# A four-layer tower on one core: the state-space sub-block takes B, C and delta straight from its normed rows, through weights multiplied together on the chip

## The chip, the cores and the metric

One core of a Trainium2 chip runs the whole program in one launch. It has TensorE (PE in the profile, with PEld its weight loads), VectorE (DVE), ScalarE (ACT), GpSimd (POOL) and SyncE (SP), which issues the direct DMAs. The metric is the device time of one execution in microseconds; lower is better. Every engine runs its instructions in order, and orders itself against the others by semaphores.

## The reference, cut to what matters

The tower turns 16 images into 16 x 36 = 576 tokens of width 256 and adds eight sub-blocks to a residual stream, each on the layer-normed stream. The third one, `L1_attn`, is the one changed. Per token row `x_in` (256 wide):

```
xz = x_in @ W_in                  # W_in 256 x 512
x, z = (xz[..., :D], xz[..., D:])
proj = x @ W_x                    # W_x 256 x (256 + 2*16)
delta_raw = proj[..., :D]; B_ssm = proj[..., D:D + N]; C_ssm = proj[..., D + N:]
delta = jax.nn.softplus(delta_raw @ W_dt + b_dt)
A = -jnp.exp(A_log)
dA = exp(delta * A); dBx = delta * x * B_ssm
h = dA_t * h + dBx_t              # along the 36 tokens of an image, 16 states per channel
y = sum over states (h * C) + x * D_param
y = y * jax.nn.silu(z) @ W_out    # then a layer norm of y + x_in, scaled and shifted
```

The sub-blocks ahead of it are a tanh recurrence (`attn0`) and a mixture of eight experts, one chosen per token (`ffn0`); behind it stand another mixture (`ffn1`) and two more layers.

## The kernel before, in words

All sub-blocks are written out one behind the other, once in each engine's program. The residual stream H and its normed copy XH lie tokens-by-partition in five tiles (four of 128 tokens, one of 64). `transpose_x(name)` on PE and `xt_copy(name)` on ACT turn XH into XT, channels by partition (2 blocks of 128 x 576 tokens). The PSUM tensor PS has 8 banks of 512 columns. A product 576 tokens wide is made in two halves of 288, each of two accumulating matmuls (k = 0, 1); the trace shows two records for one f32 matmul.

*The end of attn0 and the start of ffn0.* PE makes `token_products("attn0")`. Then `normed_residual` on DVE takes statistics of y + x, a reciprocal square root (`rsqrt`: DVE adds epsilon and signals `var_ready`, ACT takes `Sqrt` in `square_root`, line 859, DVE finishes), scales and adds, takes statistics again, and two more such roots follow. ACT's queue has only these three roots here, behind two sines. Beside that PE runs `keep_warm(11, root=4)`: 11 turns of 4 products on a zero tile, whose result nobody reads, then it waits for the fourth root and runs 5 more. After it come `transpose_x("ffn0")`, the gate's logits, the ranks, and the routed experts.

*The state-space stage* (`attn1`). PE, DVE, ACT in the order of the program:

- PE: four products of XT with `win_s` (m = 0, 1 give x, m = 2, 3 give z), banks 4 to 7, signalled by `xz_psum`; ACT copies x to `xs` and takes SiLU of z into `zs` (line 992), signalling `xz_read`.
- PE: B and C from `xs` and the last 32 columns of `wx_s`; ACT copies them to `bc_s` (line 996). SP stores them in DRAM and loads each of the 32 rows back, spread over 128 partitions (`bcB`, `bcC`, four buffers each, lines 383 to 395).
- PE: `dr`, the product of `xs` with the first 256 columns of `wx_s`; ACT copies it (line 1000); PE: its product with `wdt_s`.
- Softplus as max(v, 0) + log(1 + e^-|v|), with a correction for the rounding of 1 + e: ACT Abs with the bias (line 1005), Exp (line 1008), Ln (line 1010); DVE from line 1524 on, at full width (1152 columns for both blocks of channels), ends in `dl` (delta) and `dx` (delta times x). ACT takes exp(A_log) at line 1012.
- The loop over 16 states: DVE `input_of` (line 1549, dx times B row) and two scans (line 1557, one for each block of channels), ACT the decays for a block (line 1022, into PSUM `dA`, banks 3 to 6), POOL the product of the states with the C row (line 1170), PE the sum over states in banks 0 to 2, by products with the identity; ahead of it PE puts x times D there (`diagD`).
- DVE multiplies by `zs` (line 1571), PE makes the token products with `wout_s`.

ACT evaluates its functions from tables; the trace has a separate ACT_TABLE_LOAD wherever the next function is in another set. Its line is that of the function that it stands ahead of.

## Time and profile before

| | us |
|---|---|
| median of 3 runs | 929.83 (927.01 to 931.51) |
| profiled execution | 929.02 |
| its span | 927.2 |
| PE busy | 800.0 |
| DVE busy | 351.2 |
| ACT busy | 253.5 |
| POOL busy | 134.7 |
| mean granted clock of PE | 0.922 of full speed |

The profile is one execution, taken by the hardware profiler; times in it count from the span's start. The end of the first sub-block lies at 83 to 108, the state-space stage at 241 to 348. Busy time is the sum of an engine's instructions; a busy PE includes the idle products. The chain of waits goes back from the last instruction to what released it; a piece of it is time in which nothing else could have made the program shorter.

### The profile page before, as it was taken

The numbers are of one execution on the slowest core, as the hardware profiler recorded it, in microseconds if no ns is written. First come the engines' busy times: TensorE is split into PE (matmuls) and PEld (weight loads), VectorE is DVE, ScalarE is ACT, GpSimd is POOL, SyncE is SP. The second block draws the span as 40 slices with busy tenths as digits, with TensorE's granted clock in tenths as the row PEclk, the third lists the DMA queues.
The fourth block names the chain that finished last, engine by engine and source line by source line (L and its number), as shares of the span: only waits on it lengthen the run. The fifth ranks groups of instructions, "written<-read, shape, count | busy, mean of one in ns | idle before, by whom it ended". The sixth has DMA issues, their size and how long they took to land.

```text
span 927.2 us, 13868 instructions
## 1 busy us (share of the span) xinstructions
PE 800.0 (86%) x4994; PEld 599.6 (65%) x4994; DVE 351.2 (38%) x994; ACT 253.5 (27%) x588; POOL 134.7 (15%) x100
## 2 busy tenths in 40 slices
PE   8878779999936669998869799999998988999995
PEld 5466449897523345564544468899874556999984
DVE  1335640000359967465627641111115641111113
ACT  1222114443243321453357121222220021222210
POOL 1000020001008960023003240000013030000004
PEclk9856889999977999798999989999999978999998
DMA  9500057994034510000200064899952042899952
GB/s 336 210 2 2 1 219 262 309 318 153 20 115 117 150 28 0 1 1 0 103 0 0 1 244 138 303 322 316 309 204 84 0 163 93 276 318 317 320 179 77
DMA packets 39590, 139.27 MB, mean 150 GB/s; under 512 B 5744, under 2 KB 20288, under 8 KB 27904
## 3 DMA queue, kind: packets, MB, share of 16 engines
q1 hardware_dynamic: 37312, 132.88, 42.7%
q0 software_dynamic: 2240, 5.90, 1.9%
q8 instruction: 22, 0.36, 0.2%
q14 instruction: 16, 0.13, 0.0%
HBM read 127.40 MB, written 11.35 MB: 150 GB/s over the span
## 4 chain that ended last, share of the span: by engine, by line
PE 60%; DVE 17%; DMA 8%; issue 6%; ACT 5%; POOL 1%; another core or an unknown queue 1%; SPq 0%; DVEq 0%; POOLq 0%; ACTq 0%
PE PS L418 58%; DVE arena L1557 4%; DMA arena<-w_moe 2%; DMA arena<-x_slots 2%; DVE stats L1238 1%; DMA arena<-y_slots,posu 1%; PE PS L475 1%; PE PS L441 1%; DMA arena<-w_down 1%; ACT arena L970 1%; DVE H L1394 1%; DMA x_slots<-XH,posu 1%; DVE stats L1231 1%; DVE arena L1661 1%
## 5 line engine op out<-in xcount | busy, mean ns | idle before, releaser
L418 PE MATMUL PS<-arena 128*128 128x128 f32 (+4 forms) x3308 | 412.7, 278 | 33.5 <-ACT arena L970 9.8
L418 PEld LDWEIGHTS PS<-arena 128*128 128x128 f32 (+2 forms) x3308 | 361.7, 172 | 73.5 <-issue 19.0
L418 PE MATMUL PS<-warm 128*128 128x512 bf16 (+1 forms) x556 | 130.9, 383 | 9.7 <-DVE rs L1222 9.0
L1382 DVE TENSOR_TENSOR arena<-arena,PS 128x384 f32<-128x384 f32 (+1 forms) x62 | 30.2, 488 | 207.7 <-ACT arena L907 207.7
L418 PEld LDWEIGHTS PS<-warm 128*128 128x128 bf16 x556 | 54.6, 101 | 76.3 <-DVE rs L1222 12.8
L1157 POOL DMA_INDIRECT arena<-y_slots,posu x25 | 23.8, 951 | 389.3 <-DMA y_slots<-arena 382.6
L907 ACT ACTIVATE arena<-PS 128x384 f32<-128x384 f32 x62 | 30.4, 491 | 169.2 <-PE PS L418 169.2
L418 PE MATMUL PS<-arena,ident 128*128 128x512 f32 (+1 forms) x128 | 40.3, 462 | 37.4 <-POOL arena L1170 37.4
L1170 POOL TENSOR_TENSOR arena<-arena 128x1152 f32<-128x1152 f32 x16 | 55.9, 3491 | 49.1 <-DVE arena L1557 48.3
L418 PEld LDWEIGHTS PS<-arena,ident 128*128 128x128 f32 x128 | 21.6, 201 | 56.1 <-POOL arena L1170 39.5
L1394 DVE SCALAR_TENSOR_TENSOR H<-arena,wgt,H 128x256 f32<-128x256 f32 (+1 forms) x25 | 11.9, 477 | 121.2 <-DMA arena<-y_slots,posu 109.5
L1146 POOL DMA_INDIRECT x_slots<-XH,posu x25 | 24.1, 965 | 176.7 <-DVE posu L1342 170.0
L859 ACT ACTIVATE dev<-rs 128x5 f32<-128x5 f32 x19 | 4.1, 216 | 144.5 <-DVE rs L1222 144.5
L418 PE MATMUL PS<-XT,wsh 128*128 128x384 f32 (+1 forms) x144 | 42.2, 443 | 0.5 <-ACT arena L920 0.5
L1557 DVE TENSOR_TENSOR_SCAN arena<-PS,arena 128x576 f32<-128x576 f32 x32 | 41.5, 1339 | 0.1
L912 ACT ACTIVATE arena<-PS,arena 128x128 f32<-128x128 f32 x96 | 27.4, 368 | 42.6 <-PE PS L418 42.6
L418 PEld LDWEIGHTS PS<-XT,wsh 128*128 128x128 f32 x144 | 27.8, 207 | 12.6 <-issue 3.9
L1022 ACT ACTIVATE PS<-arena 128x560 f32<-128x560 f32 x32 | 23.3, 731 | 41.5 <-DVE arena L1557 37.3
L418 PE MATMUL PS<-arena,wsh 128*128 128x384 f32 (+1 forms) x72 | 21.9, 430 | 7.1 <-DVE arena L1370 6.8
L920 ACT ACTIVATE arena<-PS 128x256 f32<-128x256 f32 x43 | 16.5, 384 | 38.4 <-PE PS L418 38.4
L1178 POOL TENSOR_TENSOR arena<-arena,rowv 128x512 f32<-128x512 f32 (+1 forms) x12 | 13.6, 1158 | 85.6 <-ACT arena L1062 85.6
L475 PE MATMUL PS<-ident,arena 128*128 128x128 f32 x86 | 17.2, 282 | 7.0 <-DMA arena<-x_slots 4.7
(252 smaller groups left out, 761.1 us busy)
## 6 DMA issues: line engine op xcount, KB each, us to landing
arena<-w_moe SPq DMA_DIRECT2D x31, 1152.0 KB
arena<-w_moe SPq DMA_DIRECT2D x31, 1024.0 KB, 5.4
arena<-w_moe SPq DMA_DIRECT2D x24, 1026.0 KB, 6.8
arena<-bc_scratch SPq DMA_DIRECT2D x32, 288.0 KB, 3.7
arena<-x_slots SPq DMA_DIRECT2D x43, 128.0 KB, 2.2
y_slots<-arena SPq DMA_DIRECT2D x43, 128.0 KB, 5.1
wsh<-w_sh SPq DMA_DIRECT2D x1, 2176.0 KB
wl_s<-w_l SPq DMA_DIRECT2D x1, 2048.0 KB
```

The lines of the kernel that those rows point to most:

```text
L418: return nc.tensor.matmul(out_, l, r, start=start, stop=stop, skip_group_check=True)
L475: last = nc.tensor.transpose(PS[:, 6 + p, SB * d:SB * (d + 1)], xslot[p][:, 128 * d:128 * (d + 1)], ident[:, :])
L907: nc.scalar.activation(sg_s[x][:, 0:3 * SB], PS[:, 2 * x, 0:3 * SB], ACT.Silu)\
L912: last = nc.scalar.activation(hid_b[x][:, SB * c:SB * (c + 1)], PS[:, 2 * x, SB * c:SB * (c + 1)], ACT.Silu, bias=wbuf[p][:, o_ + c:o_ + c ...
L920: nc.scalar.activation(y_s[p], PS[:, 4 + p, 0:D], ACT.Copy).then_inc(sem("y_sb"), 1)
L1022: nc.scalar.activation(inner(dA[d]), inner(dl[:, d, :]), ACT.Exp, scale=A_s[:, d, bass.ds(n, 1)])\
L1146: pool.indirect_dma_start(x_slots, bass.IndirectOffsetOnAxis(ap=posu[0:TILE_N[j], k, j:j + 1], axis=0), tile(XH, j), None).then_inc(sem("s ...
L1157: pool.indirect_dma_start(Yg[0:TILE_N[j], k, j * D:(j + 1) * D], None, y_slots[0:SB * NBLK[name], :], bass.IndirectOffsetOnAxis(ap=posu[0: ...
L1170: nc.gpsimd.tensor_tensor(hC[:, n % 2, :, :], hs_[:, n % 2, :, :], bcC[:, n:n + 1, :].to_broadcast([128, KD, T]), ALU.mult)\
L1382: ins = v.tensor_tensor(hid_b[x][:, 0:full], sg_s[x][:, 0:full], PS[:, 2 * x + 1, 0:full], ALU.mult)
L1394: link(v.scalar_tensor_tensor(tile(H, j), Yg[0:TILE_N[j], k, j * D:(j + 1) * D], wgt[0:TILE_N[j], k, j:j + 1], tile(H, j), ALU.mult, ALU.add))
L1557: v.tensor_tensor_scan(hs_[:, n % 2, d], dA[d], dBx[:, n % 2, d], 0.0, ALU.mult, ALU.add)\
```

## The change

- Behind `token_products("attn0")` PE multiplies weights: it transposes the x half of `win_s` (into `winT`, which lies in YT), and makes W_in,x @ W_x and from that W_in,x @ W_x,delta @ W_dt. ACT copies each result out of PSUM, over `wx_s` and `wdt_s`, ahead of its square roots. `keep_warm(11, root=4)` becomes `keep_warm(3, root=4)`, and PE waits for the last copy before the transposes of `ffn0`.
- In the state-space stage B, C come first, then delta for channels 0 to 127 and 128 to 255 (`dt_psum` counts halves), all from XT; then the four products with `win_s`. The product for `dr` and its copy are gone. x of block 0 goes to banks 2 and 3, the other three to banks 0 and 1, one after another.
- ACT: exp(A_log) first, Abs and Exp for each half of delta, then Ln and the copy of x for each half; z is copied without SiLU, between the decays of state 0 and those of state 1. SiLU is taken of all of z behind the last decay.
- DVE: each step of delta on one half at a time, max(v, 0) in the first of them; `delta_ready` counts halves. Before the product with z it waits for SiLU.

```diff
--- before.py
+++ after.py
@@ -229,6 +229,11 @@
 
         U1 = KD * T
         xs, zs, dr, dl, dx, ys = (part(i * U1, KD, T) for i in range(6))
+        winT = YT[:, :, 0:D]
+
+        def XZ_PS(m):
+            return (PS[:, 0:2] if m else PS[:, 2:4])[:, :, 0:TH]
+
         dA = [PS[:, 3 + 2 * d:5 + 2 * d, :].rearrange("p b c -> p (b c)")[:, 0:T] for d in range(KD)]
         Y_CUT = 512
         Y_PARTS = [(0, slice(0, Y_CUT), PS[:, 0, 0:Y_CUT]), (1, slice(0, Y_CUT), PS[:, 1, 0:Y_CUT]),
@@ -637,7 +642,33 @@
             token_products("attn0", lambda k, j: HN[:, k, tsl(j)], KD, lambda k: wrnn_s[:, 2, k, :])
 
 
-            keep_warm(11, root=4)
+            def combined_weights():
+
+                pe.wait_ge(sem("ld_l1a"), 64)
+                for m in range(KD):
+                    for k in range(KD):
+                        last = nc.tensor.transpose(PS[:, 0, D * m + 128 * k:D * m + 128 * (k + 1)],
+                                                   win_s[:, k, 128 * m:128 * (m + 1)], ident[:, :])
+                last.then_inc(sem("wc_psum"), 1)
+                pe.wait_ge(sem("wc_copied"), 1)
+                for q in range(KD):
+                    for m in range(KD):
+                        last = mm(PS[:, 1, D * q:D * (q + 1)], wx_s[:, m, 128 * q:128 * (q + 1)], winT[:, m, :], m == 0, m == KD - 1)
+                last.then_inc(sem("wc_psum"), 1)
+                for k in range(KD):
+                    for m in range(KD):
+                        last = mm(PS[:, 2, 2 * NS * k:2 * NS * (k + 1)], winT[:, m, 128 * k:128 * (k + 1)],
+                                  wx_s[:, m, D:D + 2 * NS], m == 0, m == KD - 1)
+                last.then_inc(sem("wc_psum"), 1)
+                pe.wait_ge(sem("wc_copied"), 2)
+                for k in range(KD):
+                    for q in range(KD):
+                        last = mm(PS[:, 3, D * k:D * (k + 1)], wx_s[:, q, 128 * k:128 * (k + 1)], wdt_s[:, q, :], q == 0, q == KD - 1)
+                last.then_inc(sem("wc_psum"), 1)
+
+            combined_weights()
+            keep_warm(3, root=4)
+            pe.wait_ge(sem("wc_copied"), 4)
             transpose_x("ffn0")
             pe.wait_ge(sem("xt_pad"), 1)
             gate_logits("ffn0")
@@ -659,36 +690,26 @@
 
             keep_warm(14, root=5)
             transpose_x("attn1")
-            pe.wait_ge(sem("ld_l1a"), 64)
             pe.wait_ge(sem("xt_ready"), 3 * SUB["attn1"] + 3)
-            for m in range(2 * KD):
+
+            def from_xt(outs, w_of, done):
+
                 for h in range(2):
                     for k in range(KD):
-                        last = mm(PS[:, 4 + 2 * (m % 2) + h, 0:TH], win_s[:, k, 128 * m:128 * (m + 1)], XT[:, k, hsl(h)],
-                                  k == 0, k == KD - 1)
-                last.then_inc(sem("xz_psum"), 1)
+                        last = mm(outs[h], w_of(k), XT[:, k, hsl(h)], k == 0, k == KD - 1)
+                last.then_inc(sem(done), 1)
+
+            from_xt([PS[0:2 * NS, h, 0:TH] for h in range(2)], lambda k: wx_s[:, k, D:D + 2 * NS], "bc_psum")
+            for m in range(KD):
+                from_xt([PS[:, 4 + 2 * m + h, 0:TH] for h in range(2)], lambda k: wdt_s[:, k, 128 * m:128 * (m + 1)], "dt_psum")
+            for m in range(2 * KD):
                 if m == 1:
-                    pe.wait_ge(sem("xz_read"), 2)
-            for h in range(2):
-                for k in range(KD):
-                    last = mm(PS[0:2 * NS, h, 0:TH], wx_s[:, k, D:D + 2 * NS], xs[:, k, hsl(h)], k == 0, k == KD - 1)
-            last.then_inc(sem("bc_psum"), 1)
+                    pe.wait_ge(sem("bc_rows"), 2)
+                if m >= 2:
+                    pe.wait_ge(sem("xz_read"), m)
+                from_xt([XZ_PS(m)[:, h, :] for h in range(2)], lambda k: win_s[:, k, 128 * m:128 * (m + 1)], "xz_psum")
+
             pe.wait_ge(sem("xz_read"), 4)
-            for m in range(KD):
-                for h in range(2):
-                    for k in range(KD):
-                        last = mm(PS[:, 4 + 2 * h + m, 0:TH], wx_s[:, k, 128 * m:128 * (m + 1)], xs[:, k, hsl(h)],
-                                  k == 0, k == KD - 1)
-            last.then_inc(sem("dr_psum"), 1)
-            pe.wait_ge(sem("dr_ready"), 2)
-            for m in range(KD):
-                for h in range(2):
-                    for k in range(KD):
-                        last = mm(PS[:, 4 + 2 * h + m, 0:TH], wdt_s[:, k, 128 * m:128 * (m + 1)], dr[:, k, hsl(h)],
-                                  k == 0, k == KD - 1)
-            last.then_inc(sem("dt_psum"), 1)
-
-            pe.wait_ge(sem("bc_rows"), 2)
             pe.wait_ge(sem("diag_ready"), 1)
             for i, (d, ts, acc) in enumerate(Y_PARTS):
                 mm(acc, diagD[:, d, :], xs[:, d, ts], i < 3, False)
@@ -976,6 +997,17 @@
             nc.scalar.activation(cosT[:, 1:2], lru_c[:, 7:8], ACT.Sin).then_inc(sem("lru_sc"), 1)
 
 
+            act.wait_ge(sem("wc_psum"), 1)
+            nc.scalar.activation(winT, PS[:, 0, :].rearrange("p (m i) -> p m i", m=KD), ACT.Copy).then_inc(sem("wc_copied"), 1)
+            act.wait_ge(sem("wc_psum"), 3)
+            nc.scalar.activation(wx_s[:, :, 0:D], PS[:, 1, :].rearrange("p (q i) -> p q i", q=KD), ACT.Copy)\
+                .then_inc(sem("wc_copied"), 1)
+            nc.scalar.activation(wx_s[:, :, D:D + 2 * NS], PS[:, 2, 0:KD * 2 * NS].rearrange("p (k c) -> p k c", k=KD), ACT.Copy)\
+                .then_inc(sem("wc_copied"), 1)
+            act.wait_ge(sem("wc_psum"), 4)
+            nc.scalar.activation(wdt_s[:, :, :], PS[:, 3, :].rearrange("p (k f) -> p k f", k=KD), ACT.Copy)\
+                .then_inc(sem("wc_copied"), 1)
+
             xt_copy("ffn0", "rms_w", norms=3)
             gate_exp("ffn0", True)
             act.sem_inc(sem("y_sb"), 2)
@@ -985,42 +1017,45 @@
 
 
             xt_copy("attn1")
-            for m in range(4):
-                act.wait_ge(sem("xz_psum"), m + 1)
-                b = 4 + 2 * (m % 2)
-                dst = xs[:, m, :] if m < 2 else zs[:, m - 2, :]
-                nc.scalar.activation(dst.rearrange("p (h t) -> p h t", h=2), PS[:, b:b + 2, 0:TH],
-                                     ACT.Copy if m < 2 else ACT.Silu).then_inc(sem("xz_read"), 1)
+            nc.scalar.activation(A_s[:, :, :], colv[:, COL["A_log"]:COL["A_log"] + KD * NS]
+                                 .rearrange("p (k n) -> p k n", k=KD), ACT.Exp).then_inc(sem("A_exp"), 1)
             act.wait_ge(sem("bc_psum"), 1)
             for h in range(2):
                 nc.scalar.activation(bc_s[0:2 * NS, TH * h:TH * (h + 1)], PS[0:2 * NS, h, 0:TH], ACT.Copy)\
                     .then_inc(sem("bc_rows"), 1)
-            act.wait_ge(sem("dr_psum"), 1)
-            for h in range(2):
-                nc.scalar.activation(dr[:, :, TH * h:TH * (h + 1)], PS[:, 4 + 2 * h:6 + 2 * h, 0:TH], ACT.Copy)\
-                    .then_inc(sem("dr_ready"), 1)
-
-            act.wait_ge(sem("dt_psum"), 1)
             for m in range(KD):
-                nc.scalar.activation(hs_[:, 1, m].rearrange("p (h t) -> p h t", h=2), PS[:, 4 + m:8:2, 0:TH], ACT.Abs,
+                act.wait_ge(sem("dt_psum"), m + 1)
+                nc.scalar.activation(hs_[:, 1, m].rearrange("p (h t) -> p h t", h=2), PS[:, 4 + 2 * m:6 + 2 * m, 0:TH], ACT.Abs,
                                      bias=col("b_dt", m)).then_inc(sem("dt_abs"), 1)
-            act.wait_ge(sem("dt_abs"), KD)
-            nc.scalar.activation(hs_[:, 0], hs_[:, 1], ACT.Exp, scale=-1.0).then_inc(sem("dt_e"), 1)
-            act.wait_ge(sem("dt_u"), 1)
-            nc.scalar.activation(dBx[:, 1], dBx[:, 0], ACT.Ln).then_inc(sem("dt_ln"), 1)
-
-            nc.scalar.activation(A_s[:, :, :], colv[:, COL["A_log"]:COL["A_log"] + KD * NS]
-                                 .rearrange("p (k n) -> p k n", k=KD), ACT.Exp).then_inc(sem("A_exp"), 1)
+                act.wait_ge(sem("dt_abs"), m + 1)
+                nc.scalar.activation(hs_[:, 0, m], hs_[:, 1, m], ACT.Exp, scale=-1.0).then_inc(sem("dt_e"), 1)
+
+            def xz_copy(m):
+                act.wait_ge(sem("xz_psum"), m + 1)
+                dst = xs[:, m, :] if m < 2 else zs[:, m - 2, :]
+                nc.scalar.activation(dst.rearrange("p (h t) -> p h t", h=2), XZ_PS(m), ACT.Copy).then_inc(sem("xz_read"), 1)
+
+            for m in range(KD):
+                act.wait_ge(sem("dt_u"), m + 1)
+                nc.scalar.activation(dBx[:, 1, m], dBx[:, 0, m], ACT.Ln).then_inc(sem("dt_ln"), 1)
+                xz_copy(m)
             act.wait_ge(sem("A_ready"), 1)
-            act.wait_ge(sem("delta_ready"), 1)
             act.wait_ge(sem("dA_zero"), KD)
-            with act.Fori(0, NS) as n:
+
+            def decays(n):
                 for d in range(KD):
                     act.wait_ge(sem("scan_half"), 2 * n + (d + 1))
-                    act.wait_ge(sem("delta_ready"), 1)
+                    act.wait_ge(sem("delta_ready"), d + 1)
 
                     nc.scalar.activation(inner(dA[d]), inner(dl[:, d, :]), ACT.Exp, scale=A_s[:, d, bass.ds(n, 1)])\
                         .then_inc(sem("dA_ready"), 1)
+
+            decays(0)
+            for m in range(KD, 2 * KD):
+                xz_copy(m)
+            with act.Fori(1, NS) as n:
+                decays(n)
+            nc.scalar.activation(zs[:, :, :], zs[:, :, :], ACT.Silu).then_inc(sem("z_silu"), 1)
 
 
             xt_copy("ffn1", norms=2)
@@ -1519,27 +1554,33 @@
 
 
 
-            dve.wait_ge(sem("dt_abs"), KD)
+            ee, u, ln_u = hs_[:, 0], dBx[:, 0], dBx[:, 1]
             for m in range(KD):
-                mark(v.tensor_scalar(dr[:, m, :].rearrange("p (h t) -> p h t", h=2), PS[:, 4 + m:8:2, 0:TH],
-                                     col("b_dt", m), None, ALU.add))
-            join()
+                dve.wait_ge(sem("dt_abs"), m + 1)
+                v.tensor_scalar(dr[:, m, :].rearrange("p (h t) -> p h t", h=2), PS[:, 4 + 2 * m:6 + 2 * m, 0:TH],
+                                col("b_dt", m), 0.0, ALU.add, ALU.max).then_inc(sem("dt_relu"), 1)
+                dve.wait_ge(sem("dt_e"), m + 1)
+                v.tensor_scalar(u[:, m], ee[:, m], 1.0, None, ALU.add).then_inc(sem("dt_u"), 1)
+                dve.wait_ge(sem("dt_u"), m + 1)
+                link(v.scalar_tensor_tensor(ee[:, m], u[:, m], 1.0, ee[:, m], ALU.subtract, ALU.subtract))
+                dve.wait_ge(sem("dt_relu"), m + 1)
+                mark(v.tensor_tensor(dl[:, m], dr[:, m], ee[:, m], ALU.subtract))
+            dve.wait_ge(sem("A_exp"), 1)
+            v.tensor_scalar(A_s[:, :, :], A_s[:, :, :], -1.0, None, ALU.mult).then_inc(sem("A_ready"), 1)
+            dve.wait_ge(sem("xz_read"), 1)
             for d in range(KD):
                 v.memset(dA[d].rearrange("p (b l) -> p b l", l=L)[:, :, 0:1], 0.0).then_inc(sem("dA_zero"), 1)
-            ee, u, ln_u = hs_[:, 0], dBx[:, 0], dBx[:, 1]
-            dve.wait_ge(sem("dt_e"), 1)
-            v.tensor_scalar(u, ee, 1.0, None, ALU.add).then_inc(sem("dt_u"), 1)
-            dve.wait_ge(sem("dt_u"), 1)
-            link(v.scalar_tensor_tensor(ee, u, 1.0, ee, ALU.subtract, ALU.subtract))
-            link(v.scalar_tensor_tensor(dl[:, :, :], dr[:, :, :], 0.0, ee, ALU.max, ALU.subtract))
-            dve.wait_ge(sem("dt_ln"), 1)
-            link(v.scalar_tensor_tensor(ln_u, u, 1.0, ln_u, ALU.is_gt, ALU.mult))
-            v.tensor_tensor(dl[:, :, :], dl[:, :, :], ln_u, ALU.add).then_inc(sem("delta_ready"), 1)
-            dve.wait_ge(sem("A_exp"), 1)
-            v.tensor_scalar(A_s[:, :, :], A_s[:, :, :], -1.0, None, ALU.mult).then_inc(sem("A_ready"), 1)
-            dve.wait_ge(sem("delta_ready"), 1)
-            link(v.tensor_tensor(dx[:, :, :], dl[:, :, :], xs[:, :, :], ALU.mult))
-            dve.sem_inc(sem("scan_half"), 2)
+            for m in range(KD):
+                dve.wait_ge(sem("dt_ln"), m + 1)
+                link(v.scalar_tensor_tensor(ln_u[:, m], u[:, m], 1.0, ln_u[:, m], ALU.is_gt, ALU.mult))
+                v.tensor_tensor(dl[:, m], dl[:, m], ln_u[:, m], ALU.add).then_inc(sem("delta_ready"), 1)
+                if m == 0:
+                    dve.sem_inc(sem("scan_half"), 2)
+            for m in range(KD):
+                dve.wait_ge(sem("delta_ready"), m + 1)
+                dve.wait_ge(sem("xz_read"), m + 1)
+                mark(v.tensor_tensor(dx[:, m], dl[:, m], xs[:, m], ALU.mult))
+            join()
 
             def input_of(i, n):
 
@@ -1567,6 +1608,7 @@
                 if n < 3:
                     input_of(NS // 4 - 1, n + 1)
                 scan(NS // 4 - 1, n)
+            dve.wait_ge(sem("z_silu"), 1)
             dve.wait_ge(sem("hc_read"), NS + 2)
             link(v.tensor_tensor(ys[:, :, 0:Y_CUT], PS[:, 0:2, 0:Y_CUT], zs[:, :, 0:Y_CUT], ALU.mult))
             y_tail = PS[:, 2, 0:KD * (T - Y_CUT)].rearrange("p (k t) -> p k t", k=KD)
```

## Rows read from the trace of the kernel before

**Rows 1.** The page: the chain that ended last, by engine.

```profile
PE 60%; DVE 17%; DMA 8%; issue 6%; ACT 5%; POOL 1%; another core or an unknown queue 1%; SPq 0%; DVEq 0%; POOLq 0%; ACTq 0%
```

**Rows 2.** Chain of waits, state-space stage: start us, us, what.

```profile
241.42 4.13 PE PS L418 x16
...
246.28 10.30 PE PS L418 x40
...
257.84 4.16 PE PS L418 x16
262.02 1.37 ACT arena L1005 x2
263.42 1.28 ACT L1008
264.71 1.17 ACT arena L1008
...
272.33 1.31 DVE arena L1541
```

**Rows 3.** Timeline, same stage: start us, us, engine, line, operation, count, [idle before].

```profile
252.52 0.69 ACT L996 ACTIVATE arena<-PS 32x288 f32<-32x288 f32 x2 [1.41 <-PE PS L418]
...
254.92 0.37 SPq L386 DMA_DIRECT2D arena<-bc_scratch  x1
...
273.86 2.63 DVE L1549 TENSOR_TENSOR arena<-arena 128x1152 f32<-128x1152 f32 x2 [0.23 <-DVE arena L1541]
...
276.40 2.60 DVE L1557 TENSOR_TENSOR_SCAN arena<-PS,arena 128x576 f32<-128x576 f32 x2
```

**Rows 4.** Lines by form, DVE: count, busy us, mean ns, idle before.

```profile
L1524 DVE TENSOR_SCALAR arena<-PS,colv 128x576 f32<-128x576 f32 x2 | 1.5, 813 | 22.8 <-ACT arena L1005 22.8
...
L1536 DVE SCALAR_TENSOR_TENSOR arena<-arena 128x1152 f32<-128x1152 f32 x1 | 1.4, 1359 | 0.0
...
L1531 DVE TENSOR_SCALAR arena<-arena 128x1152 f32<-128x1152 f32 x1 | 0.8, 760 | 0.8 <-ACT arena L1008 0.8
...
L1708 DVE TENSOR_TENSOR arena<-arena 128x576 f32<-128x576 f32 x1 | 0.8, 757 | 0.0
```

**Rows 5.** Lines by form, ACT, same columns.

```profile
L869 ACT ACTIVATE XT<-PS 128x512 f32<-128x512 f32 x14 | 8.4, 597 | 16.6 <-PE PS L441 16.2
...
L1097 ACT ACTIVATE arena<-arena 128x576 f32<-128x576 f32 x4 | 2.7, 670 | 0.0
...
L992 ACT ACTIVATE arena<-PS 128x576 f32<-128x576 f32 x4 | 2.6, 651 | 5.9 <-PE PS L418 5.9
...
L1005 ACT ACTIVATE arena<-PS,colv 128x576 f32<-128x576 f32 x2 | 1.4, 738 | 4.2 <-PE PS L418 4.2
```

**Rows 6.** Timeline, first sub-block's norm to the gate of ffn0.

```profile
85.17 1.28 ACT L859 ACT_TABLE_LOAD   x1
...
89.77 9.67 PE L418 MATMUL PS<-warm 128*128 128x512 bf16 x44
...
92.75 0.21 ACT L859 ACTIVATE dev<-rs 128x5 f32<-128x5 f32 x1 [6.31 <-DVE rs L1222]
...
102.17 1.25 PE L418 MATMUL PS<-warm 128*128 128x512 bf16 x5 [2.74 <-DVE rs L1222]
...
107.94 2.37 PE L418 MATMUL PS<-gatew,XT 128*128 128x8 f32 x20 [0.56 <-ACT XT L874]
```

**Rows 7.** Windows, same place: PE, PEld, DVE, ACT, POOL busy us; granted clock, DMA, GB/s.

```profile
100.00:102.00 2.00, 0.00 (x0) 0.00 (x0) 1.48 (x12) 0.21 (x1) 0.00 (x0) 1.00 0.00 0
...
104.00:106.00 2.00, 2.00 (x10) 1.82 (x11) 1.14 (x4) 0.73 (x2) 0.00 (x0) 0.50 0.00 0
```

**Rows 8.** Timeline, the scan loop and its end.

```profile
290.94 3.65 POOL L1170 TENSOR_TENSOR arena<-arena 128x1152 f32<-128x1152 f32 x1 [0.26 <-DVE arena L1557]
...
334.12 5.27 POOL L1170 TENSOR_TENSOR arena<-arena 128x1152 f32<-128x1152 f32 x2 [0.26 <-DVE arena L1557]
...
343.46 4.73 PE L418 MATMUL PS<-wout_s,arena 128*128 128x256 f32 x20 [1.64 <-DVE arena L1573]
```


## The prediction

> **What bounds the kernel now.** I read the chain of waits first. Over the whole run TensorE (PE) has 60% of it, VectorE (DVE) 17%, ScalarE (ACT) 5% [rows 1]: no engine bounds it everywhere, so each stage is read by itself. In the state-space stage the chain is one long hand-over. PE does the products for x at 241.42, then in one 10.30 us piece z, B and C, and the first delta product, ACT copies, PE does the second delta product from 257.84, ACT takes absolute values at 262.02, loads a table, takes the exponential at 264.71, and DVE does five full-width steps until 273.6 [rows 2]. Only then DVE makes two scan inputs, and the first scan starts at 276.40 [rows 3]. From the first product to the first scan that is 276.40 - 241.42 = 34.98 us with one engine working at a time. After it comes the loop of 16 states, where DVE has no idle time (POOL's product waits for the scan, 0.26 us) [rows 8]; its instructions are not touched.
>
> The other place touched is the end of the first sub-block. There PE runs 44 idle products from 89.77 to 99.4 while DVE and ACT walk a norm chain; ACT's square root is taken at 92.75, the moment its input is there, because its table was loaded at 85.17 [rows 6]. That table load is hidden now.
>
> **State-space stage, after the change.** Eight records of 288 columns (four products) take half of 4.13 us, 2.06 [rows 2].
> PE: B and C come first, 241.42 to 243.5; delta rows 0 done 245.7, rows 1 done 247.7 (each with some 0.13 us of tail, as 262.02 against 257.84 + 4.06). The x products end at 249.8 and 251.7, behind them.
> ACT: A's exponential and its table load (1.28) go into the 2.3 us before B and C are ready; the B, C copies end at 244.3, against 252.52 + 0.69 = 253.2 [rows 3], so the first broadcast row is asked for 8.9 us earlier, at 246.0; DVE wants it at 257.5. Nothing to pay. Then Abs 0 from 245.7 (0.74) to 246.44, Exp 0 (0.67) to 247.13; Abs 1 from 247.75 to 248.49, Exp 1 to 249.18; Ln's table 1.28 to 250.48, Ln 0 to 251.16, x copy 0 (0.65) to 251.83, Ln 1 to 252.5, x copy 1 to 253.2 [rows 5].
> DVE starts at 246.46 and, by these times, never waits again: two PSUM reads of 0.81; two sums "1+e" that I put at 0.45 each (the full one is 0.76; its half is 0.38, and the fixed part seen below adds some 0.08); ten half-width two-operand steps at 0.757; three small steps (negating A, two memsets) that I put at 0.27 together, an estimate the sum hardly feels [rows 4]. That is 1.63 + 0.90 + 7.57 + 0.27 = 10.37, and 17 gaps of 0.03 make 10.9: x times delta ends at 257.3. Halving costs here: two halves are 1.51 where the whole is 1.36 [rows 4], 0.155 more for each of five pairs, 0.8 us in all, included. Two inputs and the wait before them are the 276.40 - 273.86 + 0.23 = 2.77 of now [rows 3]: first scan at 260.1. The gain is 276.40 - 260.1 = 16.3 us.
> Bounds: with "1+e" at 0.38 and no gaps, 17.0; with a copy of x that comes 1 us late and DVE steps some 0.05 longer, 14.7.
>
> What the new first-scan time drags along: the decay for rows 0 needs the Exp table again (253.2 to 254.5), which is before scan 0 wants it. Then x copy aside, the two z copies run at 256.3 and 259.2 and end at 259.8; the second pair of decays is wanted at 261.4, when the first half scan is done. Slack 1.6 us. PE's diagonal products follow the last z copy, 259.9 to 262.2; POOL's first product could start at 262.7. If they were late by up to 1 us the second buffer of POOL hides it. SiLU, now last on ACT: one table load (1.28) and one 1152-wide step (1.17) after the last decay, where DVE waits for POOL's last two products, 5.27, and PE behind them [rows 2, 8]: hidden with about 4 us to spare; a further load for the next square root too.
>
> **Weight products.** PE takes them up at about 89.8, where the idle products are now. ACT is in order, and its four copies, each with a wait for PE, stand ahead of the square root of 92.75 on its queue; DVE waits for that root and everything behind it waits for DVE. (PE's wait for the weights' loads, which moves here from the later stage, is for the first loads of SP's queue, and its wait for the last copy ahead of the transposes is over long before XH is there: both nothing.) So this is on the path. A record with 128 rows of weights and few columns takes 2.37/20 = 0.12 [rows 6]; one of 256 columns 0.213 (20 in 4.73 with tail) [rows 8]. Four transposes 0.6: 90.4. Copy of 512 columns 0.60 [rows 5]: 91.0. Eight records of 256 columns 1.7, eight of 32 columns 0.95, tail 0.2: 93.85. Copy 0.60: 94.45 (the small one beside PE). Eight records 1.7 and tail: 96.35. Copy: 97.0. The square root's table, which the program order now puts behind the copies (a load stands right before the first function that needs it, as the one at 263.42 behind Abs), 1.28: the root at 98.35 and not 92.75. Cost 5.6 us. Bounds: 4.3 if the load is out of the way; 9.9 if these products ran at the low clock, twice their 4.35. The granted clock is 1.00 as late as 100 to 102 [rows 7], so I stay with 5.6.
>
> **Clock after it.** Now PE idles 2.7 us before the five root products at 102.17, which take 0.25 each at full clock, and by 104 to 106 the clock is 0.50 (1.2 GHz) [rows 6, 7]. Afterwards 12 idle products end at 98.9 and the root comes at 107.8: 8.9 us idle. The five products then likely run at the low level, 2.1 us, and the transposes start 0.4 us late; they are slow already. I add 0.4, with -1.0 (the clock is back sooner) and +3 (gate products of 2.37 doubled, and some) as ends.
>
> **Sum.** -16.3 + 5.6 + 0.4 = -10.3 us. The profiled execution took 929.02 (span 927.2): 918.7. It lies 0.8 under the median of the runs, 929.83, which would give 919.5; I say 919.0.
>
> **A page on table loads.** In the trace a table load costs 1.28 and the next function starts with it done (263.42 + 1.28, next at 264.71) [rows 2]. The Trainium skill, ScalarE: Activation LUTs, section What ACT_TABLE_LOAD costs, says that each switch also drains some 1380 ns. By that rule the root is later by 1.4 and the x copies by as much; the trace does not bear it out.
>
> **Rivals.**
> 1. *The clock stays low after the long idle.* For it: 0.50 after a much shorter idle [rows 7]. Against: the same stretch is low already. If gate products and later small ones run at half rate until the experts start, +3 instead of +0.4: 921.6.
> 2. *A load costs more than it shows.* Each switch that now lies on the path takes 1.4 more: root +1.4; in the state-space stage the Ln load moves the x copies to 253.2 and DVE's memsets wait 0.9. 919.0 + 2.3 = 921.3. Against: no row has such a gap. (This is what the page above would do.)
> 3. *The detour is cheaper.* If the table load falls ahead of the copies, cost 4.3, and the clock comes back early, -1: 916.3. Against: the load at 263.42 stands behind the function before it.
> 4. *The scan loop slows: slower than before.* POOL's product takes 3.65 beside DVE but 5.27/2 = 2.6 when DVE is done, and 3.65 + 0.26 is the whole period of 3.91 [rows 8]. So POOL is as close to the bound as DVE, and what makes its product longer in the new phase lengthens all 16 states. The gain is gone when a state costs 10.0/16 = 0.63 more; at 0.9 more, 919.0 + 14.4 = 933.4. The Trainium skill, GPSIMD Engine Reference, section Specifications, has its SBUF interfaces shared with VectorE; the two durations agree. Against: the loop's own instructions and their order are the same, and by the times above both engines enter it in the same phase (POOL 0.3 after the second half scan).
> 5. *B and C rows bound the start*, so that moving them is all there is: the first row landed within 3.7 us or so of 254.92, long before 273.86 [rows 3]; near nothing for it, and it would give 925.
>
> **How the numbers follow.** Forecast 0.68, rival 1 0.13, rival 2 0.04, rival 3 0.07, rival 4 0.04, rival 5 and what I have not seen, around no change, 0.04. The forecast's own range is 916 to 922: gain 14.7 to 17.0, detour and clock 4.6 to 7, some 0.2% between executions. To take in rivals 1 to 3 and the low-clock detour (-16.3 + 9.9 + 0.4 gives 923) I go from 914.5 to 924. 0.5% is 4.6 us, about what can be told from no change; below 925.2 is faster: 0.92; same 0.04, slower 0.04.
>
> **What would show it.** First scan 18.7 us after the first product behind attn1's transposes (right), over 21 (wrong). ACT's first root in the norm after the recurrence 5 to 6 us later than the token products ask for it, with a table load just before it; if it lies within 1 us of its input, the detour was free. Granted clock in the transposes for ffn0 0.50. Period of the loop 3.91; 4.5 is rival 4. SiLU done before PE's last accumulation. The forecast is wrong if DVE shows waits over 1 us between its first delta step and the first scan.

## The result, and the profile after

| | before | changed |
|---|---|---|
| median of 4 runs each | 928.68 us | 915.04 us (911.67 to 916.38) |
| profiled execution | 929.02 | 914.04 |
| its span | 927.2 | 912.2 |

The ratio is 0.9845, 95% interval 0.9805 to 0.9884: faster, by 13.6 us where 10.8 were forecast (929.8 to 919.0). The forecast range was 914.5 to 924: the median of the changed kernel lies just inside its low end, the profiled execution just below it. A later and longer comparison, below, gives 0.9875. To see where the time went I cut both traces at instructions that every version has, and took the length of each piece:

| piece (us) | before | changed | difference |
|---|---|---|---|
| start to the last tanh of the recurrence | 83.32 | 83.27 | -0.05 |
| to ACT's next square root | 9.43 | 15.11 | +5.68 |
| to the first gate product of ffn0 | 15.19 | 15.51 | +0.32 |
| to the first state-space product | 133.48 | 133.54 | +0.06 |
| to the first scan | 34.98 | 17.53 | -17.45 |
| to the first product with `wout_s` | 67.06 | 67.15 | +0.09 |
| to the root in front of ffn2 | 182.91 | 183.65 | +0.74 |
| to the end | 400.81 | 396.45 | -4.36 |

The pieces that hold the change, rows two to six, sum to -11.3. (Row four is nearly all the first expert stage, whose instructions are the same.) The rest, -3.7, arises in stages whose instructions are the same too. What the weight products cost by themselves is read best from the place where they start, the end of the recurrence's token products: from there to the root it is 8.78 us (89.60 to 98.38), against 2.98 before (89.77 to 92.75, [rows 6]), so 5.80.

The timeline of the changed kernel around the norm behind the recurrence (start us, us, engine, line, operation; compare [rows 6]):

```profile
89.60 0.66 PE L650 MATMUL PS<-ident,win_s 128*128 128x128 f32 x4
...
90.30 0.60 ACT L1001 ACTIVATE YT<-PS 128x512 f32<-128x512 f32 x1 [5.20 <-PE PS L650]
...
93.79 0.60 ACT L1003 ACTIVATE wx_s<-PS 128x512 f32<-128x512 f32 x1 [2.90 <-PE PS L423]
...
96.47 0.60 ACT L1008 ACTIVATE wdt_s<-PS 128x512 f32<-128x512 f32 x1 [1.97 <-PE PS L423]
...
97.08 1.28 ACT L880 ACT_TABLE_LOAD   x1
98.38 0.21 ACT L880 ACTIVATE dev<-rs 128x5 f32<-128x5 f32 x1
98.62 0.19 DVE L1259 RECIPROCAL rs<-dev 128x5 f32<-128x5 f32 x1 [6.06 <-ACT dev L880]
...
107.80 2.32 PE L423 MATMUL PS<-warm 128*128 128x512 bf16 x5 [8.77 <-DVE rs L1257]
...
113.89 2.37 PE L423 MATMUL PS<-gatew,XT 128*128 128x8 f32 x20 [0.49 <-ACT XT L895]
```

The square root waits for nothing of its own: it stands behind three hand-overs between PE and ACT and a table load, and DVE is idle for 6.06 us because of it. The granted clock, over stretches of that place:

```profile
102.00:104.00 2.00, 0.00 (x0) 0.00 (x0) 1.97 (x7) 0.00 (x0) 0.00 (x0) 0.87 0.00 0
104.00:106.00 2.00, 0.00 (x0) 0.00 (x0) 1.93 (x11) 0.00 (x0) 0.00 (x0) 0.50 0.00 0
...
108.00:110.00 2.00, 2.00 (x6) 0.73 (x5) 1.81 (x8) 0.00 (x0) 0.00 (x0) 0.50 0.00 0
```

PE's five root products now start at the low level (0.50, 1.2 GHz) and take 2.32 us where they took 1.25.

The state-space stage of the changed kernel, same view (compare [rows 2, 3]):

```profile
247.43 2.13 PE L423 MATMUL PS<-XT,wx_s 128*32 128x288 f32 x8 [0.27 <-ACT XT L890]
...
249.60 0.69 ACT L1024 ACTIVATE arena<-PS 32x288 f32<-32x288 f32 x2 [0.68 <-PE PS L423]
...
253.67 0.74 ACT L1028 ACTIVATE arena<-PS,colv 128x576 f32<-128x576 f32 x1 [0.48 <-PE PS L423]
...
258.83 0.76 DVE L1576 TENSOR_TENSOR arena<-arena 128x576 f32<-128x576 f32 x1
...
259.50 0.75 DVE L1575 SCALAR_TENSOR_TENSOR arena<-arena 128x576 f32<-128x576 f32 x1
...
260.29 0.76 DVE L1576 TENSOR_TENSOR arena<-arena 128x576 f32<-128x576 f32 x1
260.97 1.42 DVE L1582 TENSOR_TENSOR arena<-arena 128x576 f32<-128x576 f32 x2
...
262.98 3.34 PE L423 MATMUL PS<-XT,win_s 128*128 128x288 f32 x8 [1.94 <-ACT arena L1036]
264.96 2.60 DVE L1598 TENSOR_TENSOR_SCAN arena<-PS,arena 128x576 f32<-128x576 f32 x2
266.36 0.65 ACT L1036 ACTIVATE arena<-PS 128x576 f32<-128x576 f32 x1 [3.43 <-PE PS L423]
266.90 1.52 ACT L1050 ACTIVATE PS<-arena 128x560 f32<-128x560 f32 x2
...
271.69 3.65 POOL L1205 TENSOR_TENSOR arena<-arena 128x1152 f32<-128x1152 f32 x1 [0.26 <-DVE arena L1598]
...
319.88 5.25 DVE L1598 TENSOR_TENSOR_SCAN arena<-PS,arena 128x576 f32<-128x576 f32 x4
...
322.70 5.27 POOL L1205 TENSOR_TENSOR arena<-arena 128x1152 f32<-128x1152 f32 x2 [0.26 <-DVE arena L1598]
...
324.65 1.16 ACT L1058 ACTIVATE arena<-arena 128x1152 f32<-128x1152 f32 x1
...
330.50 1.23 DVE L1613 TENSOR_TENSOR arena<-PS,arena 128x1024 f32<-128x1024 f32 x1 [5.38 <-PE PS L423]
```

From 252.51 to the first scan DVE has no wait. Steps that need not wait for each other start 0.67 us apart though each takes 0.76 (258.83, 259.50; 260.29, 260.97); a step that needs the result of the one before starts 0.79 behind it (259.50, 260.29). The loop's POOL product is 3.65 with 0.26 ahead of it, as in [rows 8]: the period is the same 3.91. At its end SiLU (line 1058) is done at 325.8; the DVE step that needs it starts at 330.50, behind PE's sum.

### The profile page after: what moved, and what is told of

Read it like the earlier page. It is cut to its first block, busy times and chain, and to the rows that moved or that the text cites. A ratio compares the mean times of both kernels' runs of the same rounds, so it can differ in the third digit from the quotient of the medians.

```text
span 912.2 us, 13733 instructions
## 1 busy us (share of the span) xinstructions
PE 789.5 (87%) x4886; PEld 597.3 (65%) x4974; DVE 352.1 (39%) x1000; ACT 255.4 (28%) x593; POOL 135.2 (15%) x100
## 4 chain that ended last, share of the span: by engine, by line
PE 59%; DVE 16%; DMA 9%; issue 6%; ACT 5%; POOL 4%; SPq 0%; DVEq 0%; POOLq 0%; ACTq 0%
PE PS L423 57%; DVE arena L1598 4%; DMA arena<-w_moe 3%; DMA arena<-x_slots 2%; POOL arena L1192 2%; DVE stats L1273 1%; PE PS L480 1%; POOL arena L1205 1%; PE PS L446 1%; DMA arena<-y_slots,posu 1%; DMA arena<-w_down 1%; DMA x_slots<-XH,posu 1%; ACT arena L991 1%; DVE arena L1703 1%; DVE arena L1706 1%
## 5 line engine op out<-in xcount | busy, mean ns | idle before, releaser
L423 PE MATMUL PS<-warm 128*128 128x512 bf16 (+1 forms) x436 | 117.8, 383 | 21.2 <-DVE rs L1257 15.0
L423 PEld LDWEIGHTS PS<-warm 128*128 128x128 bf16 x524 | 51.5, 101 | 79.1 <-DVE rs L1257 18.8
L423 PE MATMUL PS<-arena,ident 128*128 128x512 f32 (+1 forms) x128 | 38.0, 440 | 21.2 <-POOL arena L1205 21.2
L1213 POOL TENSOR_TENSOR arena<-arena,rowv 128x512 f32<-128x512 f32 (+1 forms) x12 | 13.6, 1158 | 86.3 <-ACT arena L1097 86.3
```

What stands on the lines that cost most here:

```text
L423: return nc.tensor.matmul(out_, l, r, start=start, stop=stop, skip_group_check=True)
L1213: nc.gpsimd.tensor_tensor(u, u, row("g2", D, e)[0:TILE_N[j], None, :].to_broadcast([TILE_N[j], n, D]), ALU.mult)\
```

## The experiments

Each kernel was timed against the kernel before on the same chip; ratios are to it. As the untouched stages turned out to vary, each verdict rests on the lengths of pieces first, on the ratio second.

**Both kernels once more.** No edit.

> The kernel before once more, unchanged, to see how far two profiled executions of one program differ stage by stage. Between the root at the start of the third layer's expert stage (526.4 in the first profile) and the end it had 400.8 us, the changed kernel 396.4. Theory A (those 4.4 us are what such a stage, which streams weights, varies by between executions): this profile lies anywhere in 396 to 403 there, while up to 526 it repeats within 0.3. Rival B (the change shortens the untouched stages for good): 400.8 again within 0.7. Ratio 1.000 within 0.2% either way.

> The changed kernel once more, unchanged. Theory A (the part of the gain beyond -11.5 us is what the untouched stages vary by between executions): the stretch from the first state-space product to the first scan repeats at 17.5 us and the norm root behind the recurrence at 98.4 within 1, while the untouched stages behind the state-space stage differ from the first profile by several us; the ratio to the kernel before, over more runs, comes to 1 - 11.4/930 = 0.988, within 0.9855 to 0.9895. Rival B (the untouched stages gain for good): 0.9845.

| | ratio | last tanh to root | root to gate | first product to first scan | attn2, root to root | rest to the end |
|---|---|---|---|---|---|---|
| before | 1 | 9.43 | 15.19 | 34.98 | 84.19 | 400.8 |
| before again | 0.9993 (0.9956 to 1.0031) | 9.34 | 15.19 | 34.99 | 89.45 | 392.7 |
| changed | 0.9845 (0.9805 to 0.9884) | 15.11 | 15.51 | 17.53 | 84.29 | 396.4 |
| changed again | 0.9875 (0.9825 to 0.9925) | 15.64 | 14.86 | 17.53 | 87.53 | 394.4 |

One program, two executions: 8 us apart behind 526, 5 us apart in one sub-block of the third layer, in opposite directions, so that their spans differ by 1. Single runs of the kernel before lay between 924.7 and 938.4. The kernel before missed both expectations: 392.7 behind 526 is below the 396 to 403 of either theory, and ahead of 526 it did not repeat within 0.3 (attn2 84.2 and 89.5). The pieces that hold the change repeat within some 0.7, the state-space piece within 0.01. So theory A's spread was too small. The ratio doesn't decide between the theories: 0.9875 was expected (0.9855 to 0.9895), and it is 11.6 us of 929.7, but rival B's 0.9845 lies in its interval too. The pieces decide it. In the second pair rows two to six sum to -11.6, and all the rest to +1.1 where the first pair had -3.7: the sign has turned, so that rest is variation and no effect of the change.

The piece from the last tanh to the root varies as well. It holds the recurrence's 20 token products, which take 6.13 to 7.73 us in the profiles of this document, the longer the later the granted clock comes back from 0.50. From the start of the weight products to the root it is 8.77 or 8.78 us in every profile that has them there, but for the one with the added square root below.

Where one sub-block (attn2, the third layer's first) differs by 5 us: PE's gate products, in the kernel before and in its second execution.

```profile
479.88 2.21 PE L418 MATMUL PS<-arena 128*128 128x288 f32 x8 [1.37 <-DVE arena L1649]
482.92 1.21 PE L418 MATMUL PS<-arena 128*128 128x288 f32 x4 [0.83 <-ACT arena L1086]
```

```profile
482.03 3.90 PE L418 MATMUL PS<-arena 128*128 128x288 f32 x8 [1.37 <-DVE arena L1649]
486.76 1.21 PE L418 MATMUL PS<-arena 128*128 128x288 f32 x4 [0.83 <-ACT arena L1086]
```

The windows over these stretches (PE, PEld, DVE, ACT, POOL busy; granted clock):

```profile
482.00:488.00 6.00, 3.80 (x16) 2.43 (x16) 1.51 (x2) 3.15 (x5) 0.00 (x0) 1.00 0.00 0
```

```profile
472.00:478.00 6.00, 3.80 (x16) 2.39 (x15) 1.52 (x2) 4.18 (x5) 0.00 (x0) 1.00 0.00 0
...
482.00:484.00 2.00, 1.97 (x5) 1.39 (x6) 0.00 (x0) 0.00 (x0) 0.00 (x0) 0.55 0.00 0
...
484.00:490.00 6.00, 3.80 (x11) 2.17 (x10) 1.51 (x2) 2.90 (x4) 0.00 (x0) 0.78 0.00 0
```

The same instructions behind the same gaps run at full clock in one execution and partly at half in the other. Over the whole sub-block its length goes, by and large, with the mean granted clock: 84.2 and 84.3 us at 0.98, 85.6 at 0.96, 87.5 to 89.2 at 0.94, 89.5 at 0.92 in the profiles of this document, while DVE is busy for 49.8 or 49.9 us in all of them. Of the 8 us behind 526, 6 lie in the last piece, from the root at 740.08 to the end: 187.1 us at a mean clock of 0.93, and 181.2 at 0.96 in the second execution.

**The weight products alone**, in the kernel before, at the changed kernel's place:

```diff
-            keep_warm(11, root=4)
+            combined_weights()          # results into YT and lam, read by nobody
+            keep_warm(3, root=4)
+            pe.wait_ge(sem("wc_copied"), 4)
...                                      # and ACT's four copies ahead of xt_copy("ffn0")
```

> The kernel before with the weight products and ACT's four copies alone, in the place where the change has them, into memory that nobody reads (keep_warm 11 to 3 as well); the state-space stage stays as it was. Theory A: the first root of the norm behind the recurrence goes from 92.75 to 98.4 (+5.6), the gate's products from 107.94 to 113.9, the first scan from 276.4 to 282.4: +6.0 us, 934.7, ratio 1.0065. Rival (PE is busy with idle products there anyway, so the products are hidden but for the table load): +1.3, 930. If a later start also shifts the expert stages of layers 3 and 4, the total is off from +6.0 by up to 4 either way while the first scan is not.

Ratio 1.0057 (1.0017 to 1.0096), +5.3 us. Last tanh to root 15.66 us, against 9.43 (0.4 of that are slower token products); from the start of the weight products to the root 8.77, against 2.98; root to gate 14.87; product to scan 34.98.

```profile
98.52 1.28 ACT L890 ACT_TABLE_LOAD   x1
99.81 0.21 ACT L890 ACTIVATE dev<-rs 128x5 f32<-128x5 f32 x1
```

The detour is on the path whole, though PE ran nothing but idle products there.

**Its table load taken off the path:**

```diff
+            nc.scalar.activation(lru_c[:, 10:11], lru_c[:, 0:1], ACT.Sqrt)
             act.wait_ge(sem("wc_psum"), 1)
```

> The changed kernel with one added ACT instruction, a square root of a spare column ahead of the four weight copies, so that the table for the norm's roots is loaded before them and not behind. Theory A (the table load of 1.28 us is on the path behind the last copy): root 2 at 97.1 instead of 98.4, 915.0 - 1.3 = 913.7, ratio 0.983. Rival (PE or DVE sets that time, or the copies reload a table): 915.0.

```profile
96.80 0.60 ACT L1010 ACTIVATE wdt_s<-PS 128x512 f32<-128x512 f32 x1 [1.97 <-PE PS L423]
97.30 0.20 ACT L880 ACTIVATE dev<-rs 128x5 f32<-128x5 f32 x1
```

The root follows the last copy at once: it starts 0.50 us behind the copy's start, 0.10 before the copy ends, where with the load between them it starts 1.91 behind (96.47, 98.38). So the load was worth 1.41 us, its own 1.28 and the lost overlap. Last tanh to root is 13.81 us, 1.30 under the first profile of the changed kernel, but that piece has 0.12 of slower token products in it. 0.983 (0.9779 to 0.9882) cannot tell 1.3 us, the piece can.

**The detour moved to where ACT is idle:**

```diff
-            combined_weights(); keep_warm(3, root=4); pe.wait_ge(sem("wc_copied"), 4)
+            keep_warm(11, root=4)
...                                      # ahead of transpose_x("attn1"):
-            keep_warm(14, root=5)
+            combined_weights()
+            keep_warm(5, root=5)
+            pe.wait_ge(sem("wc_copied"), 4)
...                                      # ACT's copies move to just ahead of xt_copy("attn1")
```

> The changed kernel with the weight products and copies moved to the end of the first expert stage, under the idle products in front of attn1 (keep_warm 14 to 5 there, 11 restored at the old place). There ACT is idle for 10 us ahead of the root (237.5 before) and PE runs idle products for 12. Theory A: products and copies take 7 us plus the table load 1.3, end before the root is wanted, and the detour costs nothing: root 2 back at 92.7, first scan 17.5 us behind the first state-space product, 915.0 - 6.0 = 909.0, ratio 0.979. Rival (the 6 us are only pushed to the other place, since PE or ACT is late there): 913 to 915.

```profile
233.08 0.60 ACT L1016 ACTIVATE wdt_s<-PS 128x512 f32<-128x512 f32 x1 [1.97 <-PE PS L423]
...
233.70 1.28 ACT L880 ACT_TABLE_LOAD   x1
...
238.42 0.21 ACT L880 ACTIVATE dev<-rs 128x5 f32<-128x5 f32 x1 [3.44 <-DVE rs L1257]
```

Here ACT waits 3.44 us for the root's input, after all copies and the load. Last tanh to root is back at 9.76, product to scan 17.53, and the expert stage in between, which now holds the weight products, is as long as before (133.6). Ratio 0.9814 (0.9761 to 0.9868), 17.3 us under the kernel before. The expected 0.979 lies in that interval, and so does the changed kernel's 0.9845: the trace shows the detour hidden, the times alone don't.

**Delta at full width:** one Exp, one Ln, DVE's steps over 1152 columns, x times delta too.

```diff
-                act.wait_ge(sem("dt_abs"), m + 1)
-                nc.scalar.activation(hs_[:, 0, m], hs_[:, 1, m], ACT.Exp, scale=-1.0).then_inc(sem("dt_e"), 1)
+            act.wait_ge(sem("dt_abs"), KD)
+            nc.scalar.activation(hs_[:, 0], hs_[:, 1], ACT.Exp, scale=-1.0).then_inc(sem("dt_e"), 1)
...                                      # the same for Ln and on DVE
```

> The changed kernel with delta's steps at full width again (1152 columns, one Exp, one Ln), all else as changed. From the rows after: Abs 1 ends 7.0 us behind the first product, Exp 8.2, Ln's table then and Ln to 10.7, DVE's last step on delta 14.9, x times delta 16.3, first scan 18.9: +1.4 us against 17.5. Rival (halving only adds DVE's fixed cost, 0.155 for each of five pairs, and hides nothing): first scan 0.8 earlier, 16.7.

```profile
249.65 2.13 PE L423 MATMUL PS<-XT,wx_s 128*32 128x288 f32 x8 [0.27 <-ACT XT L890]
...
257.86 0.76 DVE L1563 TENSOR_SCALAR arena<-arena 128x1152 f32<-128x1152 f32 x1 [0.37 <-ACT arena L1031]
...
268.27 2.60 DVE L1595 TENSOR_TENSOR_SCAN arena<-PS,arena 128x576 f32<-128x576 f32 x2
```

First product to first scan 18.62: halving is worth 1.09 us, not 1.4, and the rival's 16.7 is out. At full width DVE waits 1.12 us for the second Abs and 0.37 for Exp, 1.49 in all, and needs 9.48 for the steps up to x times delta. Halved it waits for neither and needs 9.88: 1.49 less 0.40. Ratio 0.9877 (0.9838 to 0.9917), not to be told from the changed kernel's.

**SiLU in the z copies:**

```diff
-    XZ_PS(m), ACT.Copy)
+    XZ_PS(m), ACT.Copy if m < 2 else ACT.Silu)
...
-            nc.scalar.activation(zs[:, :, :], zs[:, :, :], ACT.Silu).then_inc(sem("z_silu"), 1)
+            act.sem_inc(sem("z_silu"), 1)
```

> The changed kernel with SiLU taken in the two z copies, between the decays of state 0 and state 1, and not behind the loop. Theory A (gate last saves two table switches in the place where ACT has 1.6 us of slack): the first scan stays at 17.5 us, the decays of state 1 come 2.4 us later than 266.9 (19.5 behind the first product) and the scans of state 1, at 21.4 behind it, move to about 23, so the last scan ends 1.5 us later: +1.5. Rival (ACT is idle enough there, the switch is hidden): 0.

```profile
269.08 0.65 ACT L1036 ACTIVATE arena<-PS 128x576 f32<-128x576 f32 x1 [4.30 <-PE PS L423]
269.75 1.28 ACT L1050 ACT_TABLE_LOAD   x1
...
271.81 2.60 DVE L1598 TENSOR_TENSOR_SCAN arena<-PS,arena 128x576 f32<-128x576 f32 x2 [2.40 <-ACT PS L1050]
273.27 1.28 ACT L1050 ACT_TABLE_LOAD   x1 [0.85 <-DVE arena L1598]
...
277.18 1.28 ACT L1050 ACT_TABLE_LOAD   x1 [1.23 <-DVE arena L1598]
...
326.42 2.60 DVE L1598 TENSOR_TENSOR_SCAN arena<-PS,arena 128x576 f32<-128x576 f32 x2 [1.02 <-ACT PS L1050]
```

First scan to `wout_s` 70.57 us, against 67.15: +3.4, over twice the 1.5 expected. The delay of state 1 is 2.40: each of the two loads costs 1.4 as above, and the last z product, later and at a lower clock, takes 4.21 us where it took 3.34. And I had not seen that the load now stands inside the loop and is paid in each of the 15 turns. DVE's input step covers it in all but the last turn, which has none: 1.02 more. Taking the gate last is worth 3.4 us against this order. Ratio 0.9876 (0.981 to 0.9942), four runs.

**More idle products behind the detour** (`keep_warm(12, root=4)` for `keep_warm(3, root=4)`):

> The changed kernel with 12 turns of idle products and not 3 behind the weight products, so that PE is idle for some 1.5 us and not 8.8 ahead of the fourth root. Theory A (the long idle makes the transposes for the first gate run at the low clock, and their wait behind five slow products is the 0.3 us that the clock cost there): from root 2 to the gate's first product 13.6 us (15.5 in the changed kernel, 15.2 before, where the clock was low as well), granted clock 1.00 in the transposes; the time some 1.5 us under the changed kernel's, ratio 0.986. Rival (the clock falls whatever idle products do, or the added ones are in the way): 15.2 or more.

```profile
109.27 1.25 PE L423 MATMUL PS<-warm 128*128 128x512 bf16 x5 [1.00 <-DVE rs L1257]
```

```profile
110.00:112.00 2.00, 1.43 (x12) 0.93 (x11) 1.90 (x8) 0.13 (x1) 0.00 (x0) 1.00 0.00 0
```

The clock is 1.00 in the transposes and root to gate takes 14.14, against 15.51 and 14.86 in the two profiles of the changed kernel: 0.7 to 1.4 of the 1.9 expected. The rest is held by ACT: its six copies of XT now run back to back (1.98 us), and the gate's first product waits 0.92 for them. 0.982 (0.979 to 0.9849).

**Idle products in the third layer's gaps**, on the moved version:

```diff
+                    if m >= 1 and g != 1:
+                        idle_products(3 if g == 0 else 1, 6)
...                                      # and 6 ahead of each wait for h2_ready but the first
```

> The kernel with the weight products under attn1's idle products, and besides idle products put into the gaps where PE waits in the third layer's gate products (1 and 3 of 0.21 us in gaps of 0.8 and 1.4) and down products (6 in gaps of 2.25). There two profiles of the kernel before differ by 7 us from root to root (175.3 and 182.0), and where it is long the granted clock is 0.78 to 0.85 and not 1.00. Theory C (whether the clock falls there is what makes executions of all these kernels differ): the stretch is 175.3 or less in this profile, the spread of the runs shrinks from 13 us to some 7, and the median falls by 2 to 4 us: 910 to 912. Rival (the idle products are in the way of the real ones): 2 to 5 us longer there.

```profile
467.10 0.81 PE L423 MATMUL PS<-warm 128*128 128x512 bf16 x3
468.69 2.21 PE L423 MATMUL PS<-arena 128*128 128x288 f32 x8 [0.78 <-DVE arena L1697]
```

The real products are not delayed, and the sub-block takes 84.21; the ten profiles without filling have 84.2 to 89.5 there. But the stretch that the expectation names, from the root behind the state-space stage to the one in front of ffn2, takes 177.6 and not 175.3 or less: the excess lies ahead of attn2, where nothing was filled. Median 906.8, ratio 0.9733 (0.9693 to 0.9773), six runs within 3.8 us. The version without filling had 84.26 in its own profile, so the profiles don't show the gain. The ratio points to it, 0.9733 against 0.9814 (7.5 us, more than the 2 to 4 expected), but the two intervals still touch (0.9773, 0.9761), and the runs lie within 3.8 us where 7 were expected. The times fit theory C; no profile shows how the gain comes about.

**Both, and 13 turns behind the recurrence's token products:**

> Weight products under attn1's idle products, idle products in the gaps of the third layer's gate and down products, and 13 turns and not 11 behind the recurrence's token products. Against the version with 11 turns (907 us, ratio 0.9733): root 2 to the gate's first product 13.6 instead of 14.9 us, so 905.5, ratio 0.972, runs within 6 us of each other. Rival: no gain from the two turns, 907.

Ratio 0.9705 (0.9669 to 0.9741), median 904.99: the best version, 27 us under the kernel before. Its interval lies clear of that of the version without filling and with 11 turns (0.9761 to 0.9868). Root to gate is 14.08, 0.8 shorter and not 1.3. Its attn2 piece is 86.1: the low clock came earlier, in the up products, which have no filling (17.5 us in place of 15.8, granted clock 0.67 in the first 4 us of them). The runs lie 11 us apart, not 6 as expected, so the narrow spread of the version before did not come back.

## Why the prediction was right or wrong

**The direction and both mechanisms were right**, most terms to a few tenths. **Two steps failed**, both to the same side: the state-space term of -16.3 us was too small by 1.15, and "some 0.2% between executions" was too little for what the untouched stages do.

- *Weight products*: 5.6 forecast, 5.68 measured from the last tanh and 5.80 from the start of the weight products, all of it in front of the square root; with the products in the other place the root is back where it was, and the table load is 1.41 of it. The hand-over times (91.0, 93.85, 97.0, 98.35) came as 90.9, 93.8, 97.1, 98.4.
- *Clock*: +0.4 forecast, +0.32 in the first pair, -0.33 in the second. The five products at 2.1 us came as 2.32.
- *State-space stage*: -16.3 forecast, -17.45 measured, outside the bound of 17.0 that I gave. This is the mis-sized term. I put 17 gaps of 0.03 us between DVE's steps, as between chained full-width ones. Steps with no wait between them overlap by 0.09, so where I had 10.9 us from Abs 0 to the end of x times delta, it was 9.9; the inputs took 2.57, not 2.77. The rows of the kernel before showed such overlaps: two steps of 0.813 were busy for 1.5 together [rows 4], and the scan at 276.40 starts before the inputs end, 273.86 + 2.63 [rows 3]. What the stage gained was not taken apart further: no run has the new weights with the old order, so how much comes from the shorter chain of products and how much from the order is read from the rows alone.
- *z copies*: slack 1.6 us forecast. There was none: the last z product ran at the low clock (3.34 us in place of 2.2, granted clock 0.50 from 264), its copy ended at 267.0, and the decays of state 1, which could have begun at 266.3, began at 266.90. They were done at 268.4, still 0.45 ahead of their scan at 268.87, and the scans of state 1 follow 3.9 behind those of state 0 in every profile that keeps this order: the cover was that last margin, not the one I had counted.
- *SiLU hidden*: 4 us to spare forecast, 4.7 measured. *Loop period*: unchanged, the slower rival did not occur. *A load costs more than it shows* did not either, but for a tenth: 97.08 + 1.28, next function at 98.38, and one load removed was worth 1.41, not 1.28 + 1.4. *The reading of POOL's two durations* in the rival on the loop was off: the first of its last two products, together 5.27, starts at 322.70 while the scans run on to 325.1, and is no longer for it. The products of 3.65 are those beside which DVE makes an input (1.36). So the input step goes with the longer product, the scans don't; that it is the cause is argued, no run shows it.

**The total was larger than forecast**, 13.6 against 10.8. The local terms give 11.3 to 11.6 against the 10.3 of my sum, so one microsecond or so of the miss is local, nearly all of it from the state-space term. The other 2 are the untouched stages (-3.7 in the profiled pair, +1.1 in the next), and there the step "some 0.2% between executions" failed: that is 1.9 us, when three runs (927.0 to 931.5) were all I had to take it from. Single executions of the kernel before lie 14 us apart, and one sub-block is 84 or 89 us by the clock it is granted. With -17.45 in my sum the forecast would have been 917.9, and the low end of 914.5 left 3 us for all that varies. On which side of that end a run fell was chance: the four lay between 911.7 and 916.4, the profiled one at 914.04. Besides, the kernel before itself came out at 928.7 and not at the recorded 929.8.

What stays open: why the clock falls in one execution and not in another behind the same gaps, and what makes the first part of the stretch behind 526 take 176 to 184 us at a clock of 0.97 or 0.98 throughout.

## What to carry to other kernels

Work put under an engine's idle products is free only if everything it passes through is idle too: here PE was, but ACT's queue held a square root for which all waited, while at the end of the next stage, in front of attn1, both were idle. Ask of each copy what stands behind it in its queue, and which table that needs. Before a sum is set against a measurement, find out which untouched stages vary: two profiles of one program, cut at the same instructions, tell it, and the lengths of pieces then resolve 1 us where ratios don't resolve 4. Cut as close to the change as you can: a cut that takes in another stage's products takes in their clock, too.

## What the runs showed of the hardware

- A table load takes 1.28 us and the next function starts 0.02 us behind it. Without a load between them the next function starts 0.10 us before the one ahead ends, so taking a load out of the path was worth 1.41 us. The load is placed by the order of the program: a loop entered with another table than its body needs has the load inside, 15 times here.
- PE's clock fell to half (0.55 in 482 to 484) in a stretch where PE had been busy 3.80 of the 6.00 us from 472 at full clock, with gaps of 0.83 and 1.37 us, in some executions of a program and not in others. Three idle products in such a gap don't delay the next real one.
- Two half-width DVE steps on SBUF are 0.76 us each where the whole is 1.36; without a wait between them they start 0.67 apart, with one 0.79.
- POOL's product of 128 x 1152 takes 3.65 us where DVE makes a scan input beside it, and 2.6 beside the scans alone or with DVE idle.
